# Mean embedding and projection: a tile's columns moved to VectorE, and three steps of the start and of every tile put elsewhere

## The chip, the core and the metric

The kernel runs on one core of a Trainium2 chip. The metric is device time in microseconds, the median of several executions. PE is TensorE's matmul, PEld its weight load, DVE is VectorE, ACT ScalarE, POOL GpSimd, SP SyncE (it issues DMAs).

## The reference

```python
valid = sequence_ids < emb_table.shape[0]            # ids (1024, 200), table (12500, 512)
safe_ids = jnp.where(valid, sequence_ids, 0)
seq_emb = emb_table[safe_ids] * valid[..., None]
denom = jnp.maximum(valid.sum(axis=1, keepdims=True), 1.0)
user_repr = seq_emb.sum(axis=1) / denom              # (1024, 512)
logits = user_repr @ proj_w + proj_b                 # (512, 12500), (12500,)
```

Ids run from 35 to 109962, so about one in nine is valid (some 23 of 200). All arrays are float32 (ids int32).

## The kernel before

Users are split into 8 tiles of 128 (one per partition), the 12500 items into 25 weight tiles of 500. VectorE sorts each tile's valid ids to the front (`sort`, five rounds of eight). POOL then gathers table rows, one indirect DMA per column: column j of tile t brings the j-th valid row of all 128 users, for 26 columns (c = 26 t + j), into a ring of 12 buffers. Some users have more than 26 valid ids; the tile's rest of these (up to 128 rows) is listed by three small PE products (`list_rest`), gathered as one more column into `rest_rows`, and added by `sum_rest`. For more still there is a loop behind a branch on a count (`add_further`), which every tile has to test; `sum_further` waits for the columns so far and calls it.

A column is added to its tile's sum in one of two ways. PE multiplies it by a diagonal mask built on ScalarE and accumulates in the PSUM tile `turned` (`sum_column`); VectorE multiplies by the mask and adds into `sums` (`add_column`). `ON_PE` says which columns PE takes: all of tile 0, 18 to 25 of tile 1, 24 and 25 of tile 2. VectorE then makes the mean from `sums` and ScalarE's `rest_mean` (`mean_of`), PE transposes it into `turned` (`turn`, L758), and ScalarE and VectorE split it into a high and a low half.

The projection runs in 200 units (one weight tile by one user tile), in the order of a list made when the program is built: tile 0 alone first (units 0 to 9), then further tiles join at units 10, 22, 35, 51, 65, 81 and 98 (`joined`). A unit is 12 matmuls (L829) into one of 6 PSUM banks. ScalarE or VectorE moves a bank out (`move_out`; ScalarE's units get their bias by one more matmul, L834, VectorE adds `bias_sb`, L635), and SP stores it. VectorE also makes the low halves of weight tiles (`w_low`, L620).

Every engine has a queue of its own, in the order of the loops over units; `column_due` spreads a tile's columns over the units before it joins. POOL's queue holds nothing but gathers from 5.8 us on. SP's holds, first, ids, weight tiles 0 to 4 and four bias tiles, then per unit its store, weight load and bias load. At the end of tile 1's and tile 2's VectorE columns stands `sum_further`, three units before the tile joins; `mean_of` follows one unit later for tiles 1 and 2 and at once for the others. `rest_share` and `sum_rest` come two units ahead for tiles with columns on PE, three for the others.

Of the kernel before, what the change touches and what calls it, by code (L numbers as in the profile page):

```python
# [5 lines left out]
def mean_embedding_projection(nc, ids, table, proj, bias, out, FAST=26,  # L6
# [8 lines left out]
    TILES = USERS // P  # L15
# [11 lines left out]
    RAW, SPLIT, BIAS, ROWS, PLACED, BANKS = 2, 5, 4, 12, 2, 6  # L27
    CH = 2

    ON_PE, DIAGS = ((0, FAST), (18, FAST), (24, FAST)), 4  # L30
    RAW_MORE, MORE_LOADS = 2, 16
    ACT_TILES, BOTH_TILES = 1, 5
    PART_AT = (0, 32, 64)
    BIAS_ROWS = PART_AT[-1] + NB
# [25 lines left out]
    UNITS = len(units)  # L60
# [21 lines left out]
    dve_last = [max((c for c in range(FAST * t, FAST * (t + 1)) if not by_pe[c]), default=None) for t in range(TILES)]  # L82
    assert all(at % CH == 0 for pair in ON_PE for at in pair)

    GATHER_LEAD = 5
    LATE_LOAD, REST_FIRST_AT, OPENED = 7, 18, SPLIT - 1

# [9 lines left out]
    ONCE = RAW + RAW_MORE  # L97
# [13 lines left out]
    with ctx:  # L111
# [163 lines left out]
            return first_diags[c] if c < FAST else diag[:, nth[c] % DIAGS]  # L275

        def list_of(t):
            return turned if t else first_list

        @block.sync  # L280
        def _(sp):
            def load_w(q):
                if raw_last[q] is not None:
                    sp.wait_ge(s_w_lo, raw_last[q] + 1)
                sp.dma_start(raw(q), w_view[:, :, bass.ts(q % NB, BW)]).then_inc(s_raw[raw_slot[q]], 16)

            def load_bias(i):

                if i >= BIAS:
                    wait_moved(sp, late_last[i - BIAS])  # L290
                sp.dma_start(bias_sb[:, i % BIAS], bias_view[late[i] % NB:late[i] % NB + 1].to_broadcast([P, BW])).then_inc(
                    s_bias[i % BIAS], 16)

            def store(g):
                r, q, first, n = stores[g]
                wait_moved(sp, r + n - 1)
                sp.dma_start(out_view[:, first:first + n, bass.ts(q % NB, BW)],
                             stage[:, g % STAGE, 0:n]).then_inc(s_stored[g % STAGE], 16)

            sp.dma_start(ids_sb[:, 0], ids_view[:, 0]).then_inc(s_ids0, 16)  # L300
            sp.dma_start(ids_sb[:, 1:], ids_view[:, 1:]).then_inc(s_ids, 16)
            for q in range(RAW):
                load_w(q)
            sp.wait_ge(s_bias_zero, 1)
            for at in PART_AT:
                sp.dma_start(bias_raw[at:at + NB], bias_view).then_inc(s_bias_raw, 16)
            first_loads = [q for q in range(LOADS) if raw_last[q] is None or raw_last[q] < SPLIT]
            for q in first_loads[RAW:]:
                if q == LATE_LOAD:
                    sp.wait_ge(s_rows[(FAST - 1) % ROWS], 16 * ((FAST - 1) // ROWS + 1))  # L310
                load_w(q)
                if q == ONCE:
                    for i in range(BIAS):
                        load_bias(i)
            sp.wait_ge(s_bias_parts, 3)
            for r in range(UNITS):
                for g in range(len(stores)):
                    if stores[g][0] + stores[g][3] - 1 == r:
                        store(g)
                for q in range(len(first_loads), LOADS):  # L320
                    if split_due[raw_last[q]] == r:
                        load_w(q)
                for i in range(BIAS, len(late)):
                    if r == late_last[i - BIAS]:
                        load_bias(i)
            for i in range(STAGE):
                sp.wait_ge(s_stored[i], 16 * len(range(i, len(stores), STAGE)))
# [162 lines left out]
        def _(dve):  # L490
# [90 lines left out]

            def sum_further(t):
                if t:
                    dve.wait_ge(s_summed, nth[dve_last[t]] + 1)
                else:
                    dve.memset(sums[:], 0.0).then_inc(s_cleared, 1)
                    dve.wait_ge(s_cleared, 1)
                add_further(t)
# [8 lines left out]
                                         ALU.add).then_inc(s_mean, 1)  # L597

            def mean_of(t):
                dve.wait_ge(s_turned, t)  # L600
                dve.wait_ge(s_rest_mean, t)
                dve.scalar_tensor_tensor(mean[:], sums[:], inv_count[:, t:t + 1], rest_mean[:], ALU.mult,  # L602
                                         ALU.add).then_inc(s_mean, 1)
# [120 lines left out]
            for r in range(UNITS):  # L724
                if not by_act[r]:
                    move_out(r)
                if r and r in joined[:-1]:
                    fill_slots(joined.index(r) + 1)
                for q in range(SPLIT, LOADS):
                    if split_due[q] == r:  # L730
                        w_low(q)
                for t in range(1, len(ON_PE)):
                    if r + 2 == joined[t]:
                        mean_of(t)
                for c in range(FAST, COLS):
                    if not by_pe[c] and column_due(c) == r and c >= FAST + 4:
                        add_column(c)
                        t, j = divmod(c, FAST)
                        if 1 < t and t + 1 < TILES and j in SORT_NEXT:
                            sort(t + 1, SORT_NEXT.index(j))  # L740
                        if t + 1 < TILES and j == (SELECT_NEXT if t > 1 else 15):
                            choose(t + 1)
                for t in range(1, TILES):
                    if r + MEAN_AHEAD == joined[t]:
                        sum_further(t)
                        if t >= len(ON_PE):
                            mean_of(t)
                if r + TURN_AHEAD + 1 in joined[1:]:
                    mean_low(joined.index(r + TURN_AHEAD + 1))

        @block.tensor
        def _(pe):
# [8 lines left out]
            def list_rest(t):  # L761

                pe.wait_ge(s_select, 2 * t + 2)
                if t:
                    pe.wait_ge(s_mean_lo, t)
                place_in = list_of(t)
                nc.tensor.transpose(place_in[:, 0:P], select[:], ident[:])
                nc.tensor.matmul(place_in[:, VALUES:VALUES + REST], select[:], top[:, t, FAST:SORTED], start=True, stop=True)
                nc.tensor.matmul(place_in[:, PLACE:PLACE + 1], select[:], before[:, t:t + 1],
                                 start=True, stop=True).then_inc(s_listed, 1)  # L770
# [25 lines left out]
            for c in pe_columns[0]:  # L796
                if c == REST_FIRST_AT:
                    sum_rest(0)
                sum_column(c)
            turn(0)  # L800
            pe.wait_ge(s_bias_parts, 3)
            pe.wait_ge(s_pick, 2)
            for r in range(UNITS):
                for t in range(1, TILES):
                    if r == (column_due(FAST * t + ON_PE[t][0]) if t < len(ON_PE) else joined[t] - REST_AHEAD):
                        sum_rest(t)
                for c in range(FAST, COLS):
                    if by_pe[c] and column_due(c) == r:
                        sum_column(c)
                if r + TURN_AHEAD in joined[1:]:  # L810
                    turn(joined.index(r + TURN_AHEAD))
                q, t = units[r]
                if r == 0:
                    pe.wait_ge(s_w_lo, OPENED)
                if r == first_unit[q]:
                    pe.wait_ge(s_w_lo, q + 1)
                if r >= BANKS:
                    wait_moved(pe, r - BANKS)
                bank = acc[:, r % BANKS, 0:BW]
                if r == joined[t]:  # L820
                    pe.wait_ge(s_mean_hi, t + 1)
                for part in range(3):
                    if r == joined[t] and part == 2:
                        pe.wait_ge(s_mean_lo, t + 1)
                    for k in range(K):
                        hi, lo = (x[:, t, k * P:(k + 1) * P] for x in (mean_hi, mean_lo))
                        high, low = (x[:, q % SPLIT, k] for x in (w_hi, w_lo))
                        first, second = ((hi, high), (hi, low), (lo, high))[part]
                        last = nc.tensor.matmul(bank, first, second, start=part + k == 0,  # L829
                                                stop=part == 2 and k == K - 1 and not by_act[r])  # L830
                if r in joined[:-1]:
                    list_rest(t + 1)
                if by_act[r]:
                    last = nc.tensor.matmul(bank, pick[:, q % NB:q % NB + 1].to_broadcast([BIAS_ROWS, P]), bias_parts[:],  # L834
                                            start=False, stop=True)
                last.then_inc(s_product, 1)
# [22 lines left out]
```

## Time and profile before

| what | us |
|---|---|
| median of 3 runs (lowest, highest) | 640.46 (640.25, 640.85) |
| profiled execution, whole / span | 641.41 / 639.7 |
| PE busy | 609.9 (95%) |
| PEld busy | 477.1 (75%) |
| DVE busy | 407.6 (64%) |
| POOL busy | 230.1 (36%) |
| ACT busy | 145.5 (23%) |
| DMA | 158.31 MB, mean 247 GB/s |

Busy shares are means over a start in which gathers, sorting and splitting go on and a long second half of nothing but units. The granted clock is TensorE's, 1.00 being 2.4 GHz and 0.5 being 1.2 GHz.

### The profile page before, as it was taken

The numbers are of one execution on the slowest core, as the hardware profiler recorded it, in microseconds if no ns is written. First come the engines' busy times: TensorE is split into PE (matmuls) and PEld (weight loads), VectorE is DVE, ScalarE is ACT, GpSimd is POOL, SyncE is SP. The second block draws the span as 40 slices with busy tenths as digits, with TensorE's granted clock in tenths as the row PEclk, the third lists the DMA queues.
The fourth block names the chain that finished last, engine by engine and source line by source line (L and its number), as shares of the span: only waits on it lengthen the run. The fifth ranks groups of instructions, "written<-read, shape, count | busy, mean of one in ns | idle before, by whom it ended". The sixth has DMA issues, their size and how long they took to land.

```text
span 639.7 us, 7596 instructions
## 1 busy us (share of the span) xinstructions
PE 609.9 (95%) x2602; PEld 477.1 (75%) x2602; DVE 407.6 (64%) x723; ACT 145.5 (23%) x161; POOL 230.1 (36%) x227
## 2 busy tenths in 40 slices
PE   1989899999999999999999999999999999999997
PEld 0327558678787777788788788888888888888886
DVE  7988959989879698797785554332333333344442
ACT  8917525131140131300200221111011111211210
POOL 5777877767765667565550000000000000000000
PEclk9999999989999999999999999999999999999999
DMA  9989999989999889798793398454555555566632
GB/s 310 388 292 371 391 369 314 367 285 323 309 327 314 272 289 309 231 329 246 233 334 112 97 290 276 122 177 157 170 173 177 176 177 176 170 192 203 219 124 106
DMA packets 77703, 158.31 MB, mean 247 GB/s; under 512 B 9287, under 2 KB 65042, under 8 KB 77658
## 3 DMA queue, kind: packets, MB, share of 16 engines
q1 hardware_dynamic: 60378, 110.30, 51.0%
q0 software_dynamic: 17280, 47.47, 23.2%
q8 instruction: 21, 0.34, 0.2%
q14 instruction: 24, 0.20, 0.1%
HBM read 115.70 MB, written 51.20 MB: 261 GB/s over the span
## 4 chain that ended last, share of the span: by engine, by line
PE 76%; DVE 14%; issue 5%; DMA 3%; DVEq 1%; ACT 0%; POOL 0%; POOLq 0%
PE acc L829 72%; DVE sums L557 6%; DMA rows<-in_L_rec_emb_table_dram,index 3%; DVE w_lo L620 3%; PE turned L783 2%; DVE key L514 1%; DVE top L510 1%; PE turned L758 1%; PE acc L834 1%; PE turned L775 1%; DVE stage L635 1%; DVE mean L602 0%; POOL rows L349 0%; DVEq L255 0%; DMA ids_sb<-in_r_sequence_ids_dram 0%
## 5 line engine op out<-in xcount | busy, mean ns | idle before, releaser
L349 POOL DMA_INDIRECT rows<-in_L_rec_emb_table_dram,index x208 | 220.4, 1060 | 94.7 <-issue 57.0
L829 PE MATMUL acc<-w_hi,mean_hi 128*128 128x500 f32 x800 | 224.7, 402 | 0.8 <-ACT mean_hi L434 0.8
L635 DVE TENSOR_TENSOR stage<-acc,bias_sb 128x500 f32<-128x500 f32 x162 | 109.2, 676 | 181.8 <-PE acc L829 181.5
L829 PE MATMUL acc<-w_lo,mean_hi 128*128 128x500 f32 x800 | 214.7, 390 | 0.0
L829 PE MATMUL acc<-w_hi,mean_lo 128*128 128x500 f32 x800 | 214.3, 390 | 0.2 <-DVE mean_lo L607 0.2
L829 PEld LDWEIGHTS acc<-w_hi,mean_lo 128*128 128x128 f32 x800 | 150.7, 189 | 32.2 <-DVE mean_lo L607 1.2
L829 PEld LDWEIGHTS acc<-w_lo,mean_hi 128*128 128x128 f32 x800 | 150.8, 189 | 31.4
L829 PEld LDWEIGHTS acc<-w_hi,mean_hi 128*128 128x128 f32 x800 | 150.3, 189 | 32.0 <-issue 4.3
L557 DVE SCALAR_TENSOR_TENSOR sums<-rows,mask,sums 128x512 f32<-128x512 f32 x165 | 124.0, 752 | 8.2
L418 ACT ACTIVATE w_hi<-w_raw 128x2000 fp32r<-128x2000 f32 x39 | 72.9, 1875 | 232.6 <-PE acc L829 215.8
L620 DVE TENSOR_TENSOR w_lo<-w_raw,w_hi 128x1000 fp32r<-128x1000 f32 x74 | 85.2, 1193 | 10.5 <-ACT w_hi L418 10.5
L409 ACT ACTIVATE stage<-acc 128x500 f32<-128x500 f32 x38 | 22.2, 586 | 82.8 <-PE acc L834 82.8
L445 ACT ACTIVATE rest_mean<-turned,inv_count 128x512 f32<-128x512 f32 x7 | 4.8, 689 | 77.6 <-PE turned L775 68.9
L783 PE MATMUL turned<-rows,diags_at_hi 128*128 128x512 f32 x30 | 16.0, 692 | 1.3 <-DMA rows<-in_L_rec_emb_table_dram,index 1.3
L510 DVE MAX8 top<-key 128x8 f32<-128x200 f32 x40 | 14.6, 366 | 0.7
L834 PE MATMUL acc<-bias_parts,pick 89*128 89x500 bf16 x38 | 14.6, 385 | 0.0
L602 DVE SCALAR_TENSOR_TENSOR mean<-sums,inv_count,rest_mean 128x512 f32<-128x512 f32 x7 | 5.3, 751 | 14.2 <-issue 7.1
L514 DVE MATCH_REPLACE8 key<-top,key 128x200 f32<-128x200 f32 x40 | 14.1, 352 | 0.0
L783 PEld LDWEIGHTS turned<-rows,diags_at_hi 128*128 128x128 f32 x30 | 6.5, 224 | 10.0 <-issue 7.6
L783 PE MATMUL turned<-rows,diag 128*128 128x512 f32 x20 | 10.2, 624 | 3.7 <-ACT diag L402 2.1
L783 PE MATMUL turned<-rows,diags_at_lo 128*128 128x512 f32 x22 | 11.5, 628 | 1.7 <-DMA rows<-in_L_rec_emb_table_dram,index 1.4
L434 ACT ACTIVATE mean_hi<-turned 128x512 fp32r<-128x512 f32 x8 | 4.8, 597 | 34.8 <-PE turned L758 34.8
(106 smaller groups left out, 180.4 us busy)
## 6 DMA issues: line engine op xcount, KB each, us to landing
out_dram<-stage SPq DMA_DIRECT2D x200, 250.0 KB, 3.7
w_raw<-in_L_rec_proj_w_dram SPq DMA_DIRECT2D x39, 1000.0 KB, 6.5
bias_sb<-in_L_rec_proj_b_dram SPq DMA_DIRECT2D x39, 250.0 KB, 4.6
raw_at_hi<-in_L_rec_proj_w_dram SPq DMA_DIRECT2D x4, 1000.0 KB, 10.1
rows<-in_L_rec_emb_table_dram,index POOLq DMA_INDIRECT x208, 5.8
raw_at_lo<-in_L_rec_proj_w_dram SPq DMA_DIRECT2D x3, 1000.0 KB, 14.3
stage<-in_L_rec_proj_w_dram SPq DMA_DIRECT2D x1, 1000.0 KB, 26.2
ids_sb<-in_r_sequence_ids_dram SPq DMA_DIRECT2D x1, 700.0 KB, 4.6
```

Of the source, the lines that this page charges most:

```text
L349: return pool.indirect_dma_start(out=dst, out_offset=None, in_=table, in_offset=bass.IndirectOffsetOnAxis(ap=column, axis=0), bounds_check ...
L409: nc.scalar.activation(stage[:, g % STAGE, r - stores[g][0]], acc[:, r % BANKS, 0:BW], ACT.Copy).then_inc(s_moved_by_act, 1)
L418: nc.scalar.activation(w_hi[:, q % SPLIT], raw(q), ACT.Copy).then_inc(s_w_hi, 1)
L510: dve.max(eight, key[:]).then_inc(s_sort, 1)
L514: dve.match_replace(key[:], eight, key[:], -1.0).then_inc(s_sort, 1)
L557: dve.scalar_tensor_tensor(sums[:], rows[:, c % ROWS], mask[:, t, j:j + 1], sums[:], ALU.mult, ALU.add).then_inc(s_summed, 1)
L620: low = dve.tensor_tensor(w_lo[:, q % SPLIT, at:at + half], raw(q)[:, at:at + half], high, ALU.subtract)
L635: dve.tensor_tensor(stage[:, g % STAGE, r - stores[g][0]], acc[:, r % BANKS, 0:BW], bias_sb[:, i % BIAS], ALU.add).then_inc(s_moved_by_dve, 1)
L758: last = nc.tensor.transpose(turned[:, k * P:(k + 1) * P], mean[:, k * P:(k + 1) * P], ident[:])
L783: nc.tensor.matmul(turned[:], diagonal_of(c), rows[:, c % ROWS], start=j == 0, stop=j == FAST - 1).then_inc(s_added, 1)
L829: last = nc.tensor.matmul(bank, first, second, start=part + k == 0, stop=part == 2 and k == K - 1 and not by_act[r])
L834: last = nc.tensor.matmul(bank, pick[:, q % NB:q % NB + 1].to_broadcast([BIAS_ROWS, P]), bias_parts[:], start=False, stop=True)
```

## The change

Tile 2 has no columns on PE any more; VectorE adds all 26 and, as `ON_PE` has one entry less, its mean is made three units ahead, right behind its last column, and its rests are added three units ahead too. The test for further rows moves from behind a tile's last VectorE column to behind column 20 (16 for tile 1), and `mean_of` waits for the last column instead. The four first bias loads move on SP from behind weight tile 4 to unit 3. Tile 1's list of rests moves on PE from unit 0 to ahead of column 21 of tile 0, and from `turned` into the PSUM bank of unit 5, which then waits until the list was read.

```diff
-    ON_PE, DIAGS = ((0, FAST), (18, FAST), (24, FAST)), 4
+    ON_PE, DIAGS = ((0, FAST), (18, FAST)), 4
+    FURTHER_BEHIND, LIST_FIRST_AT, BIAS_DUE = 20, 21, 3
+    further_behind = [min(FURTHER_BEHIND, pe_columns[t].start - 2) if pe_columns[t] else FURTHER_BEHIND
+                      for t in range(TILES)]
         def list_of(t):
-            return turned if t else first_list
+            return turned if t > 1 else first_list
...
-                if q == ONCE:
+            sp.wait_ge(s_bias_parts, 3)
+            for r in range(UNITS):
+                if r == BIAS_DUE:
                     for i in range(BIAS):
                         load_bias(i)
-            sp.wait_ge(s_bias_parts, 3)
-            for r in range(UNITS):
...
             def sum_further(t):
                 if t:
-                    dve.wait_ge(s_summed, nth[dve_last[t]] + 1)
+                    dve.wait_ge(s_summed, nth[FAST * t + further_behind[t]] + 1)
             def mean_of(t):
+                dve.wait_ge(s_summed, nth[dve_last[t]] + 1)
...
                         add_column(c)
                         t, j = divmod(c, FAST)
+                        if j == further_behind[t]:
+                            sum_further(t)
...
                 for t in range(1, TILES):
-                    if r + MEAN_AHEAD == joined[t]:
-                        sum_further(t)
-                        if t >= len(ON_PE):
-                            mean_of(t)
+                    if t >= len(ON_PE) and r + MEAN_AHEAD == joined[t]:
+                        mean_of(t)
...
             def list_rest(t):
                 pe.wait_ge(s_select, 2 * t + 2)
-                if t:
+                if t == 1:
+                    pe.wait_ge(s_placed, 1)
+                    pe.wait_ge(s_rest_index, 1)
+                elif t:
                     pe.wait_ge(s_mean_lo, t)
...
                 if c == REST_FIRST_AT:
                     sum_rest(0)
+                if c == LIST_FIRST_AT:
+                    list_rest(1)
                 sum_column(c)
...
+                if r == BANKS - 1:
+                    pe.wait_ge(s_placed, 2)
+                    pe.wait_ge(s_rest_index, 2)
...
-                if r in joined[:-1]:
+                if r and r in joined[:-1]:
                     list_rest(t + 1)
```

## Rows read from the trace of the kernel before

**Rows 1.** The page, part 4: shares of the chain that ended last, by engine.

```profile
PE 76%; DVE 14%; issue 5%; DMA 3%; DVEq 1%; ACT 0%; POOL 0%; POOLq 0%
```

**Rows 2.** PE's waits: who waited for whom, us in total, times, longest.

```profile
PE turned L758 <- DVE mean L602: 3.6, 3, 1.9
PE turned L783 <- DMA rows<-in_L_rec_emb_table_dram,index: 4.3, 6, 1.3
```

**Rows 3.** Timeline of PE at tile 2: start, us, operation, [idle before <-releaser].

```profile
121.80 1.02 PE L775 MATMUL turned<-rest_rows,placed 128*128 128x512 f32 x2
122.66 1.92 PE L783 MATMUL turned<-rows,diag 128*128 128x512 f32 x4
124.01 1.47 PE L829 MATMUL acc<-w_hi,mean_hi 128*128 128x500 f32 x4
...
129.39 0.66 PE L758 MATMUL turned<-ident,mean 128*128 128x128 f32 x4 [1.88 <-DVE mean L602]
```

**Rows 4.** Stretches: length, busy PE, PEld, DVE, ACT, POOL, clock, DMA share, GB/s.

```profile
76.00:80.00 4.00, 2.81 (x6) 1.06 (x6) 3.96 (x7) 2.69 (x8) 3.10 (x3) 1.00 1.04 393
96.30:127.10 30.80, 30.80 (x131) 23.55 (x130) 29.72 (x54) 11.56 (x13) 23.48 (x23) 1.00 0.98 338
128.00:132.00 4.00, 2.61 (x11) 2.25 (x12) 3.13 (x6) 0.79 (x2) 3.01 (x4) 0.82 1.00 357
132.00:136.00 4.00, 4.00 (x16) 3.23 (x15) 3.77 (x10) 0.00 (x0) 3.00 (x3) 0.75 0.95 326
```

**Rows 5.** Timeline of DVE from tile 2's list to its mean.

```profile
96.33 0.22 DVE L572 TENSOR_SCALAR rank<-turned,own_slot 128x1 f32<-128x1 f32 x1 [1.18 <-PE turned L769]
...
99.39 0.68 DVE L635 TENSOR_TENSOR stage<-acc,bias_sb 128x500 f32<-128x500 f32 x1
...
123.38 2.46 DVE L557 SCALAR_TENSOR_TENSOR sums<-rows,mask,sums 128x512 f32<-128x512 f32 x3
...
126.34 0.75 DVE L557 SCALAR_TENSOR_TENSOR sums<-rows,mask,sums 128x512 f32<-128x512 f32 x1
128.58 0.75 DVE L602 SCALAR_TENSOR_TENSOR mean<-sums,inv_count,rest_mean 128x512 f32<-128x512 f32 x1 [1.49 <-issue]
```

**Rows 6.** Timelines of DVE and PE at tile 6, and of PE at 7.

```profile
302.46 0.68 DVE L635 TENSOR_TENSOR stage<-acc,bias_sb 128x500 f32<-128x500 f32 x1 [2.23 <-PE acc L829]
...
305.27 0.75 DVE L602 SCALAR_TENSOR_TENSOR mean<-sums,inv_count,rest_mean 128x512 f32<-128x512 f32 x1 [1.47 <-issue]
...
306.08 0.66 PE L758 MATMUL turned<-ident,mean 128*128 128x128 f32 x4 [1.02 <-DVE mean L602]
...
355.15 0.66 PE L758 MATMUL turned<-ident,mean 128*128 128x128 f32 x4 [0.73 <-DVE mean L602]
```

**Rows 7.** Timelines of PE and DVE at tile 3.

```profile
162.96 1.02 PE L775 MATMUL turned<-rest_rows,placed 128*128 128x512 f32 x2
163.41 1.48 PE L829 MATMUL acc<-w_hi,mean_hi 128*128 128x500 f32 x4
...
168.92 0.75 DVE L602 SCALAR_TENSOR_TENSOR mean<-sums,inv_count,rest_mean 128x512 f32<-128x512 f32 x1 [0.95 <-DVE sums L557]
...
169.73 0.66 PE L758 MATMUL turned<-ident,mean 128*128 128x128 f32 x4
```

**Rows 8.** DVE's waits.

```profile
DVE mean L602 <- ACT rest_mean L445: 6.2, 1, 6.2
```

**Rows 9.** Timeline: ACT's copy of tile 1's list, PE's unit 5.

```profile
54.25 0.28 ACT L439 ACTIVATE placed<-turned 128x128 f32<-128x128 f32 x1 [3.00 <-DVE rest_index L579]
...
64.73 1.25 PE L829 MATMUL acc<-w_hi,mean_hi 128*128 128x500 f32 x4
```

**Rows 10.** Timeline of SP's DMA issues.

```profile
7.58 14.30 SPq L291 DMA_DIRECT2D bias_sb<-in_L_rec_proj_b_dram  x4
```

**Rows 11.** POOL's gathers by line, from 54 to 80 us, then 24 to 40 us.

```profile
L349 POOL DMA_INDIRECT rows<-in_L_rec_emb_table_dram,index x17 | 21.1, 1240 | 5.2 <-issue 4.6 <-DVE sums L557 0.6
...
L349 POOL DMA_INDIRECT rows<-in_L_rec_emb_table_dram,index x12 | 12.0, 997 | 3.7 <-issue 2.4 <-PE turned L783 1.2
```

More of the change, by code:

```diff
@@ L83, in mean_embedding_projection @@
     assert all(at % CH == 0 for pair in ON_PE for at in pair)
+    further_behind = [min(FURTHER_BEHIND, pe_columns[t].start - 2) if pe_columns[t] else FURTHER_BEHIND
+                      for t in range(TILES)]
+    assert all(by_pe[FAST * t + j] is False and j >= FAST - ROWS for t, j in enumerate(further_behind) if t)
     GATHER_LEAD = 5
```

## The prediction

> **What bounds the kernel now.** I read the page's chain of waits first, for the engine on which the end hangs. It gives TensorE (PE) three quarters of the span and VectorE (DVE) most of the rest [rows 1]. After that I asked where PE stands still, because a microsecond of PE waiting, once its units run, is a microsecond of the end. PE's waits name two causes that this change touches: the transposes of a mean (L758) wait 3.6 us for VectorE in three places, and the diagonal products of table rows (L783) wait 4.3 us for gathers in six places [rows 2]. Third, the timelines around those places.
>
> At tile 2 PE leaves the sum of the rests at 121.80, does two columns from 122.66, starts unit 20 at 124.01, finishes it at 129.39 - 1.88 = 127.51 and then waits 1.88 us for the mean [rows 3]. VectorE is what is late there. From 96.30 to 127.10 it is busy for 29.72 of 30.80 us [rows 4], and its last wait for another engine, 1.18 us for PE's list of tile 2, ends at 96.33 [rows 5]. So from 96.33 until the mean at 128.58 this stage is one uninterrupted VectorE queue, and PE has time to spare in it. At tiles 6 and 7 the picture is the other one: VectorE itself waits 2.23 us for a product, adds the last column, tests for further rows and only then makes the mean; PE stands 1.02 us at 306.08 and 0.73 us at 355.15 for it [rows 6]. 1.88 + 1.02 + 0.73 are the 3.6 us of PE's waits, so tiles 3, 4 and 5 have no such wait of size.
>
> **The change part by part.** Durations are of the profiled execution, which took 641.41 us (span 639.7 and 1.7 around it), 0.95 us over the median of 640.46. I add the terms to 641.41 and take 0.95 off at the end.
>
> *Tile 2's two columns.* PE loses two columns. At tile 3, which has none, a unit follows the sum of the rests by 163.41 - 162.96 = 0.45 us [rows 7]; at tile 2 by 124.01 - 121.80 = 2.21 [rows 3]. So PE is 1.76 us earlier at the end of unit 20. This is worth nothing by itself: PE would only wait longer, since VectorE is the late one. ScalarE's two diagonals go too, off the path. VectorE gains two columns. Three in a row take 2.46 us from the first's start to the last's end [rows 5], so the pitch is (2.46 - 0.75) / 2 = 0.855, and two more are 1.71 us on a queue with no gap. Their rows were gathered for PE before 124.01, so VectorE doesn't wait for them at 127 or later. Term: +1.71 at tile 2's mean.
>
> *The test for further rows, tile 2.* It moves from behind the last column to behind column 20. It costs VectorE the time from the end of the last column, 126.34 + 0.75 = 127.09, to the mean at 128.58: 1.49 us, with some 0.1 that any dependent step takes [rows 5]. It waits for column 20's sum before it loads its register, so it empties the queue at the new place as at the old, and behind it stand the remaining columns and bank moves. VectorE has no idle time there to hide it [rows 4]. Term: 0. The same step takes 0.95 at tile 3 [rows 7], so at the new place it could be 0.54 cheaper; the other end is as dear as any of its rows, 1.49. Range -0.5 to +0.1.
>
> *The test, tiles 6 and 7.* Behind column 20 it lies in time in which VectorE waits for products anyway (2.23 us just ahead of the last column [rows 6]). The mean then starts right after the last column, about 1.4 us earlier than 305.27, and PE needs it only 1.02 us earlier. Both waits go: -1.02 - 0.73 = -1.75. What is late next is PE itself. At tiles 4 and 5 PE doesn't wait for the mean, so 0. At tile 1 the mean waits 6.2 us for ScalarE's share of the rests [rows 8], which hides the test at either place.
>
> *The test, tile 3.* Mean and transposes follow with no gap: the mean ends at 168.92 + 0.75 = 169.67, the transposes begin at 169.73 [rows 7]. The stage is VectorE-bound like tile 2's, and the test stays in it. Term 0, from -0.1 to +0.5 (0.95 against 1.49).
>
> *The clock behind tile 2's wait.* From 128 to 136 the granted clock is 0.82 and then 0.75 [rows 4], that is, 1.2 GHz for part of it, after PE's wait of 1.88 us: 4 x 0.18 + 4 x 0.25 = 1.72 us of PE work lost. The wait grows to 1.88 + 1.76 + 1.71 = 5.35 us. No row shows so long a wait between units. At the least the loss goes (-1.72, since the shorter waits for rows before 87 us show a clock of 1.00, as in 76 to 80 [rows 4]); at the most it doubles. The nearest row is the same place, so I take the same loss: 0.
>
> *Tile 1's list and the waits that come with it.* PE makes it at column 21 of tile 0, where the rows of the gathers keep PE waiting (the 4.3 us [rows 2]), so three small products fit in. It waits for tile 0's list to have been used and for the choice on VectorE, both done long before; behind it in PE's queue stand only the last five columns. The new wait at unit 5 (at 64.73) is for a copy that ScalarE began at 54.25 [rows 9]: ten microseconds of cover. Unit 0 gets shorter by them, but PE waits for gathered rows ahead of unit 8 in any case, so the gain is lost there. Term: 0.
>
> *The first bias loads.* SP spends 14.30 us from 7.58 on issuing four of them [rows 10]. Without them the first loads and gathers have the DMA engines more to themselves, and unit 0 may start up to a microsecond earlier, which again ends at the rows that unit 8 waits for. At the new place, unit 3, they stand on SP ahead of that unit's store and weight load and all later ones, whose banks and buffers are used again many units on; their own first user is VectorE's bank move at 99.39 [rows 5], 34 us after even unit 5 (64.73) began. Term: 0.
>
> *What sets unit 8.* The gathers leave POOL one behind another. From 54 to 80 they take 1240 ns each, from 24 to 40 they take 997 [rows 11]: 17 x 0.243 = 4.1 us lost, beside seven pairs of low-half subtractions (L620) on VectorE, 0.6 us a pair. If VectorE's work shifts against POOL's, a pair more or less is hit: 0, from -0.6 to +0.6.
>
> **Sum.** 641.41 + 1.71 (columns) + 0 (test, tile 2) + 0 (clock) + 0 (tile 3) + 0 (start) - 1.75 (tiles 6 and 7) = 641.37; less 0.95: 640.4 us. Gain and loss cancel.
>
> **The rivals.** *A: the test at tile 2 leaves the path.* If VectorE has a gap near column 20 after all (PE's earlier units, or a longer wait for a bank), the test is swallowed and the mean comes only 1.71 - 1.39 = 0.32 later. For it: at tiles 6 and 7 it is so. Against it: 29.72 of 30.80 us busy [rows 4]. Time: 641.41 + 0.32 - 1.75 - 0.95 = 639.0.
>
> *B: the longer wait costs more clock.* It lies at unit 21; it decides if TensorE, after a wait nearly three times as long, works at 1.2 GHz for twice as long. Price: another 1.72, which VectorE doesn't hide, because it waits for the list that PE makes at the head of tile 2's units. Time: 640.4 + 1.7 = 642.1. For it: the drop was there after 1.88 us already. Against it: part of a low stretch may pass while PE still waits, which costs nothing.
>
> The Trainium skill, "TensorE: Matmul & The Clock Gate", section "What's actually happening", says that the throttled state is the default and that activity releases it. The 0.82 and 0.75 behind PE's wait agree [rows 4]. By that rule the loss is sure after 5.35 us of waiting and less sure after 1.88; if the median run before was without it, the rule would give 642.1 where the rows of the profiled execution give 640.4.
>
> *C: the bias loads hurt where they go.* From 76 to 80 the DMA share is 1.04 at 393 GB/s [rows 4]. Four loads write 1 MB, 1.0 / 0.393 = 2.6 us of it. If the last two gathers of tile 1 are held up by that much, unit 8 and all behind it come 2.6 us later: 643.0. It decides if the gathers queue behind the loads. Against it: the DMA engines are as full now, and gathers pass.
>
> **How the numbers follow.** Forecast 0.52, A 0.22, B 0.16, C 0.10. What this measurement can tell from no change is 0.2%, 1.3 us. The forecast's own range is 639.2 to 641.8, from its open terms (test, tile 3, start, part of the clock), so of its 0.52 I count 0.40 within, 0.08 faster and 0.04 slower. A gives 0.18 faster and 0.04 within; B 0.12 slower and 0.04 within; C 0.09 slower and 0.01 within. Faster 0.26, same 0.49, slower 0.25. The range reaches to A with its cheapest test and to B, and stops short of C: 638.5 to 642.6.
>
> **What would show it.** In the profile after: PE's two columns at tile 2 gone; the wait of L758 for tile 2's mean about 5 us instead of 1.88, and that mean about 1.7 us later than 128.58; a granted clock below 1 right after it; no wait of L758 at tiles 6 and 7; unit 8 at the same time as before to about half a microsecond. I am wrong if tile 2's mean is not later (A), if the low clock behind it lasts clearly longer (B), if tile 1's last columns wait longer for rows (C), or if the waits at tiles 6 and 7 stay.

## The result, and the profile after

The changed kernel takes 641.87 us (median of 20 runs, 640.57 to 643.30), the kernel before 640.60 (20 runs, 640.08 to 641.00). The ratio is 1.0020, 95% interval 1.0014 to 1.0026: 1.3 us slower (0.9 to 1.7), where I had forecast no change. The profiled executions hide this: 641.41 us before and 641.37 after. The one of before lies above all 20 runs of before, the one of after half a microsecond under the median of after.

In the profile after, the lines of before have moved: the turn of a mean is L763 (was L758), the mean L607, a column on VectorE L561, the unit's products L842, the columns on PE L791, the sum of the rests L783, the bank move L640. The shares of the chain have hardly changed [rows 1]:

```profile
PE 77%; DVE 13%; DMA 4%; issue 4%; ACT 0%; DVEq 0%; POOL 0%; POOLq 0%
```

PE's waits (total, times, longest), against [rows 2]. Three waits for a mean have become two, and one of them is three times as long; the waits for rows are shorter, and one for a diagonal stands beside them:

```profile
PE turned L763 <- DVE mean L607: 5.9, 2, 5.7
PE turned L791 <- ACT diag L406: 3.5, 1, 3.5
PE turned L791 <- DMA rows<-in_L_rec_emb_table_dram,index: 2.8, 5, 1.0
```

PE at tile 2, against [rows 3]. The unit follows the rests by 0.46 us, with no columns between. PE ends it at 125.24, 2.27 sooner than before, and then waits until 130.92, so the turn is 1.53 later. The four products behind it take 2.02 us where the same four took 1.48 at 119.00:

```profile
118.54 1.02 PE L783 MATMUL turned<-rest_rows,placed 128*128 128x512 f32 x2
119.00 1.48 PE L842 MATMUL acc<-w_hi,mean_hi 128*128 128x500 f32 x4
...
130.92 1.11 PE L763 MATMUL turned<-ident,mean 128*128 128x128 f32 x4 [5.68 <-DVE mean L607]
131.69 2.02 PE L842 MATMUL acc<-w_hi,mean_hi 128*128 128x500 f32 x4
```

Stretches (columns as in [rows 4]): VectorE's from tile 2's list to its mean, and the two in which the granted clock was 0.82 and 0.75 before. It is now 0.56 and 0.59, near the lower of the two levels (1.2 GHz); in the first of them PE works for only 1.08 of 4.00 us:

```profile
95.80:130.11 34.31, 29.44 (x128) 22.94 (x127) 31.55 (x56) 11.55 (x12) 25.33 (x25) 0.98 1.00 357
128.00:132.00 4.00, 1.08 (x5) 1.08 (x6) 3.68 (x6) 0.00 (x0) 3.09 (x4) 0.56 0.92 318
132.00:136.00 4.00, 4.00 (x13) 3.21 (x12) 3.79 (x11) 0.60 (x1) 3.04 (x4) 0.59 0.96 342
```

VectorE over that time, against [rows 5]. The test for further rows now stands between column 20 (122.89) and a bank move, and VectorE is idle for 1.27 us there instead of 1.49 just ahead of the mean. From the list's answer to the mean are 34.31 us, 2.06 more than the 32.25 before:

```profile
95.80 0.22 DVE L576 TENSOR_SCALAR rank<-turned,own_slot 128x1 f32<-128x1 f32 x1 [1.19 <-PE turned L777]
...
96.60 0.76 DVE L561 SCALAR_TENSOR_TENSOR sums<-rows,mask,sums 128x512 f32<-128x512 f32 x1
97.26 0.36 DVE L514 MAX8 top<-key 128x8 f32<-128x200 f32 x1
...
101.68 2.47 DVE L561 SCALAR_TENSOR_TENSOR sums<-rows,mask,sums 128x512 f32<-128x512 f32 x3
104.06 0.36 DVE L514 MAX8 top<-key 128x8 f32<-128x200 f32 x1
...
122.89 0.75 DVE L561 SCALAR_TENSOR_TENSOR sums<-rows,mask,sums 128x512 f32<-128x512 f32 x1
124.92 0.68 DVE L640 TENSOR_TENSOR stage<-acc,bias_sb 128x500 f32<-128x500 f32 x1 [1.27 <-issue]
125.51 3.32 DVE L561 SCALAR_TENSOR_TENSOR sums<-rows,mask,sums 128x512 f32<-128x512 f32 x4
...
129.33 0.75 DVE L561 SCALAR_TENSOR_TENSOR sums<-rows,mask,sums 128x512 f32<-128x512 f32 x1
130.11 0.75 DVE L607 SCALAR_TENSOR_TENSOR mean<-sums,inv_count,rest_mean 128x512 f32<-128x512 f32 x1
```

Tile 6 on VectorE, then tiles 6 and 7 on PE, against [rows 6]. The mean follows the last column with no test between, and neither turn has a wait any more:

```profile
304.59 0.68 DVE L640 TENSOR_TENSOR stage<-acc,bias_sb 128x500 f32<-128x500 f32 x1 [1.75 <-PE acc L842]
305.19 0.75 DVE L561 SCALAR_TENSOR_TENSOR sums<-rows,mask,sums 128x512 f32<-128x512 f32 x1
305.97 0.75 DVE L607 SCALAR_TENSOR_TENSOR mean<-sums,inv_count,rest_mean 128x512 f32<-128x512 f32 x1
```

```profile
307.03 0.60 PE L763 MATMUL turned<-ident,mean 128*128 128x128 f32 x4
...
355.14 0.60 PE L763 MATMUL turned<-ident,mean 128*128 128x128 f32 x4
```

### The profile page after: what moved, and what is told of

Its sections match the earlier page's. It is cut to its first block, busy times and chain, and to the rows that moved or that the text cites. A ratio compares the mean times of both kernels' runs of the same rounds, so it can differ in the third digit from the quotient of the medians.

```text
span 639.6 us, 7590 instructions
## 1 busy us (share of the span) xinstructions
PE 607.6 (95%) x2598; PEld 477.7 (75%) x2598; DVE 409.5 (64%) x725; ACT 145.0 (23%) x159; POOL 229.2 (36%) x227
## 4 chain that ended last, share of the span: by engine, by line
PE 77%; DVE 13%; DMA 4%; issue 4%; ACT 0%; DVEq 0%; POOL 0%; POOLq 0%
PE acc L842 72%; DVE sums L561 5%; DMA rows<-in_L_rec_emb_table_dram,index 4%; DVE w_lo L625 3%; PE turned L791 2%; DVE key L518 1%; DVE top L514 1%; PE turned L783 1%; PE acc L847 1%; PE turned L763 1%; DVE stage L640 0%; DMA ids_sb<-in_r_sequence_ids_dram 0%; DVE count L652 0%; ACT w_hi L422 0%; POOL rows L353 0%
## 5 line engine op out<-in xcount | busy, mean ns | idle before, releaser
L640 DVE TENSOR_TENSOR stage<-acc,bias_sb 128x500 f32<-128x500 f32 x162 | 109.3, 676 | 183.3 <-PE acc L842 181.7
L842 PE MATMUL acc<-w_hi,mean_hi 128*128 128x500 f32 x800 | 225.1, 403 | 0.8 <-ACT mean_hi L438 0.8
L842 PE MATMUL acc<-w_lo,mean_hi 128*128 128x500 f32 x800 | 214.7, 390 | 0.0
L842 PE MATMUL acc<-w_hi,mean_lo 128*128 128x500 f32 x800 | 213.8, 389 | 0.2 <-DVE mean_lo L612 0.2
L842 PEld LDWEIGHTS acc<-w_hi,mean_hi 128*128 128x128 f32 x800 | 150.7, 190 | 32.0 <-issue 4.3
L842 PEld LDWEIGHTS acc<-w_hi,mean_lo 128*128 128x128 f32 x800 | 150.4, 188 | 32.0 <-DVE mean_lo L612 1.1
L842 PEld LDWEIGHTS acc<-w_lo,mean_hi 128*128 128x128 f32 x800 | 150.8, 189 | 31.4
L561 DVE SCALAR_TENSOR_TENSOR sums<-rows,mask,sums 128x512 f32<-128x512 f32 x167 | 125.5, 752 | 15.3 <-issue 6.7
L791 PE MATMUL turned<-rows,diags_at_hi 128*128 128x512 f32 x30 | 15.5, 661 | 1.8 <-DMA rows<-in_L_rec_emb_table_dram,index 1.8
L791 PEld LDWEIGHTS turned<-rows,diags_at_hi 128*128 128x128 f32 x30 | 6.1, 214 | 10.5 <-issue 5.4
L791 PE MATMUL turned<-rows,diag 128*128 128x512 f32 x16 | 9.1, 721 | 4.0 <-ACT diag L406 3.5
L353 POOL DMA_INDIRECT rest_rows<-in_L_rec_emb_table_dram,rest_index x8 | 8.2, 1031 | 12.9 <-DVE sums L561 7.9
L763 PE MATMUL turned<-ident,mean 128*128 128x128 f32 x32 | 5.4, 296 | 7.3 <-DVE mean L607 5.9
```

The lines of the kernel that those rows point to most:

```text
L353: return pool.indirect_dma_start(out=dst, out_offset=None, in_=table, in_offset=bass.IndirectOffsetOnAxis(ap=column, axis=0), bounds_check ...
L561: dve.scalar_tensor_tensor(sums[:], rows[:, c % ROWS], mask[:, t, j:j + 1], sums[:], ALU.mult, ALU.add).then_inc(s_summed, 1)
L640: dve.tensor_tensor(stage[:, g % STAGE, r - stores[g][0]], acc[:, r % BANKS, 0:BW], bias_sb[:, i % BIAS], ALU.add).then_inc(s_moved_by_dve, 1)
L763: last = nc.tensor.transpose(turned[:, k * P:(k + 1) * P], mean[:, k * P:(k + 1) * P], ident[:])
L791: nc.tensor.matmul(turned[:], diagonal_of(c), rows[:, c % ROWS], start=j == 0, stop=j == FAST - 1).then_inc(s_added, 1)
```

## The experiments

Two theories stood at the start. *Q*: tile 2's columns cost more than the earlier test gives back, by VectorE's later mean and by the low clock behind PE's longer wait. *S*: the moves at the start (bias loads, tile 1's list) cost it. The table is of use for all runs; a *turn* is the transposing of a tile's mean on PE. From each profile: VectorE's time from tile 2's list to its mean; from turn 1 to turn 2 on PE; PE's wait ahead of turn 2; from turn 2 to turn 3, where PE waits at most 0.76 us for the next mean, so that a low clock shows; from turn 3 to turn 7, which holds the tests at tiles 4 to 7. Then the ratio to the kernel before by the timed runs, 0.001 being 0.64 us. Last, how far the profiled run lies from the median of its own kernel, in us: as far as the differences that are argued here. The largest of these go with where turn 1 begins (88.40 and 88.80 in e10 and e9; 90.07, 90.46 and 90.48 in e4, e11 and e1), so only stretches from there on are compared. Each is of a single execution, and VectorE's idle time at tile 2's test alone is anything from 1.23 to 1.81 us in them.

| kernel | list to mean | turn 1 to 2 | wait at 2 | turn 2 to 3 | turn 3 to 7 | ratio (95%) | profiled run, from median |
|---|---|---|---|---|---|---|---|
| before | 32.25 | 39.81 | 1.88 | 40.34 | 185.42 | 1 | +0.81 |
| after | 34.31 | 41.88 | 5.68 | 40.99 | 183.23 | 1.0020 (1.0014–1.0026) | -0.50 |
| e1 after, tile 2 back on PE | 32.03 | 39.59 | 0.52 | 39.75 | 183.26 | 0.9968 (0.9956–0.9980) | +1.00 |
| e2 before, tile 2 on VectorE | 34.53 | 42.11 | 5.90 | 41.13 | 185.44 | 1.0060 (1.0047–1.0073) | +0.37 |
| e3 after, wait filled | 34.66 | 42.23 | 1.15 | 39.66 | 183.27 | 0.9999 (0.9988–1.0009) | +0.51 |
| e4 after, banks on ScalarE | 32.72 | 40.29 | 2.97 | 40.82 | 183.25 | 0.9979 (0.9968–0.9989) | +1.35 |
| e5 before, start moved | 32.00 | 39.57 | 1.26 | 39.45 | 185.55 | 0.9995 (0.9986–1.0004) | +0.66 |
| e6 before, test moved | 32.51 | 40.08 | 0.99 | 39.65 | 183.24 | 0.9982 (0.9973–0.9991) | -0.41 |
| e7 before, wait filled | 32.05 | 39.61 | none | 39.37 | 185.36 | 1.0001 (0.9992–1.0010) | -0.29 |
| e8 e1 and e4 | 30.16 | 38.83 | none | 39.63 | 183.30 | 0.9950 (0.9936–0.9963) | 0.00 |
| e9 after, columns short | 33.24 | 40.80 | 4.57 | 40.33 | 183.24 | 0.9997 (0.9987–1.0007) | -1.13 |
| e10 e1, VectorE work added | 33.89 | 41.45 | 2.68 | 40.69 | 183.32 | 1.0009 (1.0001–1.0018) | -1.19 |
| e11 after, no test at tile 2 | 32.93 | 40.48 | 4.26 | 41.57 | 183.31 | 0.9994 (0.9985–1.0002) | +1.77 |
| e12 after again | 34.34 | 41.89 | 5.67 | 40.66 | 183.31 | 1.0020 (1.0008–1.0031) | -0.64 |

**The parts one by one: e1, e2, e5, e6.** e1 takes only tile 2's columns out of the change, e2 does nothing but them:

```diff
-    ON_PE, DIAGS = ((0, FAST), (18, FAST)), 4
+    ON_PE, DIAGS = ((0, FAST), (18, FAST), (24, FAST)), 4
```

> The changed kernel with tile 2's columns 24 and 25 given back to TensorE (its mean again two units ahead); the test, the bias loads and the list stay moved. Theory Q (VectorE's queue): tile 2's two columns are all that costs, and the moved test gives back what the profiles show at tiles 5 to 7, 2.1 us. Then 640.6 - 2.1 = 638.5 us. Rival S (the start): the moved bias loads or list cost about the 1.3 us that the whole change cost, through later gathers for unit 8; then tile 2 is neutral and this kernel stays between 640 and 642 us.

> The kernel before with only ON_PE changed: VectorE adds all of tile 2's columns and its mean comes three units ahead, the test behind the last column as before. Theory Q: tile 2's mean about 2 us later and PE's wait about 5.5 us instead of 1.9, with 0.5 to 1.4 us more lost at 1.2 GHz behind it: 640.6 + 2.0 + 0.5 to 1.4 = 643.1 to 644.0 us. Rival S: the two columns cost nothing net, 640.6 plus or minus 0.5 us.

e1 took 638.31 us against 640.33, e2 644.11, 0.1 beyond its range. So the columns alone cost 3.8 us (0.0060), and without them the change gains 2.0; put into the rest of the change they cost 3.3 (1.0020 against 0.9968). S is refuted: what is left of the change when the columns are back is faster than before.

e5 makes only the moves at the start (the bias loads at unit 3, tile 1's list at column 21 with its waits), e6 only that of the test:

```diff
-                    dve.wait_ge(s_summed, nth[dve_last[t]] + 1)
+                    dve.wait_ge(s_summed, nth[FAST * t + further_behind[t]] + 1)
...
+                        if j == further_behind[t]:
+                            sum_further(t)
```

> Before, with the first bias loads and tile 1's list moved as in the change, and nothing else of it. Theory Q (tile 2's queue and clock cost, the earlier test gains): unit 8 starts 0.52 us earlier in the changed kernel's trace, and tile 2's mean, which VectorE sets, follows from tile 1's end, so 0 to -0.5 us, 639.8 to 640.4 us against 640.3 before. Rival S (the start costs): +1 us, about 641.3. Rival R (the start is what gained the 2 us by which the change with tile 2's columns put back beats before): 638.3 us.

> Before, with the test for further rows moved behind column 20 (behind an earlier one where TensorE adds the columns) and nothing else of the change. Theory Q: the waits ahead of turns 6 and 7 (1.02 and 0.73 us before) go, and tile 2's own test leaves the place just ahead of its mean, where it cost 1.49 us, for one in mid-queue, where it costs about 1.3: -1.75 to -2.1 us, 638.2 to 638.6 us. Rival R (the start gained the 2 us): 640.0 to 640.4 us.

e5: 639.94 against 640.52, not to be told from no change (+0.3 to -0.9 us). e6: 639.39, that is -1.2 us (-0.6 to -1.7), less than the 1.75 to 2.1 expected, though its profile shows what the theory says: turn 3 to 7 is 2.18 shorter. The profile of before is not the one to measure it by (more on that below). Against e7's, which is before without its wait at tile 2, turn 1 to 2 is 0.47 longer in e6 (the test took 1.81 us there, 1.27 in e7), turn 2 to 3 0.28 longer and turn 3 to 7 2.12 shorter: together 1.4 us, within the interval. Rival R, that the start gained the 2 us, fell.

**The clock: e3 and e7.** In both, PE gets products of a unit whose sums are overwritten, in place of its wait at tile 2, and the columns stay where they are. e3 adds 22 to the changed kernel, e7 adds 7 to the one before:

```diff
+                if r + TURN_AHEAD == joined[2]:
+                    wait_moved(pe, r - BANKS)
+                    pe.wait_ge(s_w_lo, q + 1)
+                    for _ in range(22):
+                        nc.tensor.matmul(acc[:, r % BANKS, 0:BW], mean_hi[:, t, 0:P], w_hi[:, q % SPLIT, 0],
+                                         start=True, stop=True)
```

> The changed kernel with 22 more matmuls of unit 21 (about 5 us at 2.4 GHz) ahead of tile 2's transposes, in the wait for its mean; they are overwritten by the unit's own. The mean comes no sooner, only the granted clock behind the wait should stay at 1.00. Theory K (the clock is a large part): what PE lost at 1.2 GHz after the wait, 2.1 us in the profiled execution, comes back: 641.9 - 2.1 = 639.8 us. Rival (the clock is cheap, because VectorE is the late engine in the stage that follows): less than 0.7 us comes back, 641.2 us or more.

> Before, with seven further matmuls of a unit, whose sums are overwritten, in TensorE's queue ahead of tile 2's turn, so that it works through most of the 1.88 us for which it waited there. Theory Q: the granted clock of the stretch 128 to 140 us is 1.00 in every run; 12 of before's 20 runs have a mean clock of 1.000 as it is, so the median gains 0 to 0.4 us, 639.9 to 640.4 us. Rival (the low clock costs before about as much as the changed kernel, 1.7 us, in its typical run): 638.6 us.

e3: 640.08, ratio 0.9999, nearer to theory K's 639.8 than to its rival's 641.2. The whole loss is gone, although VectorE's mean is not sooner (list to mean 34.66) and PE does more. Its timeline of PE and its stretch behind the turn:

```profile
125.08 5.20 PE L825 MATMUL acc<-w_hi,mean_hi 128*128 128x500 f32 x22
131.42 0.66 PE L763 MATMUL turned<-ident,mean 128*128 128x128 f32 x4 [1.15 <-DVE mean L607]
131.83 1.16 PE L848 MATMUL acc<-w_hi,mean_hi 128*128 128x500 f32 x4
```

```profile
132.00:136.00 4.00, 4.00 (x20) 3.30 (x18) 3.69 (x12) 0.60 (x1) 3.09 (x4) 1.00 0.98 363
```

PE does the four products in 1.16 us where they took 2.02, at a granted clock of 1.00, and turn 2 to turn 3 falls from 40.99 to 39.66. e7, the same cure for the kernel before, gains nothing: 640.67 against 640.52, ratio 1.0001 (0.9992 to 1.0010), a little over the 640.4 expected at most. So the kernel before has no such loss in its typical run, or one of at most 0.5 us. Two stretches of e7:

```profile
76.00:80.00 4.00, 3.44 (x5) 1.53 (x6) 3.96 (x7) 1.70 (x6) 3.13 (x3) 0.62 1.04 391
132.00:136.00 4.00, 3.98 (x21) 3.03 (x20) 3.79 (x10) 0.00 (x0) 3.08 (x4) 1.00 1.02 344
```

The clocks of the runs say the same: 12 of the 20 runs of before beside e1 to e4 have a mean granted clock of 1.000 (their median is 640.18, that of the other eight, at 0.997, 640.51), while all 20 of the changed kernel stand at 0.989 or 0.992, and the 12 of e3 at 0.994 to 0.997. In the two later sets of runs of before 23 of 62 stand at 0.999 or 1.000, with medians 0.2 and 0.3 under those of the others; a mean below that needn't come from behind turn 2, since e7's profile has 0.997 and its low stretch from 76 to 80 us (0.62), where PE waits for rows anyway. The profiled execution of before was one with a drop behind turn 2. e5, whose tile 2 is before's, shows one without: 1.26 us of wait, a clock of 1.00 from 128 to 140, 39.45 from turn 2 to 3.

**VectorE's load and PE's queue apart: e4, e9, e10, e11.** e4 moves the banks of tile 1's units on ScalarE, with the bias by a product on PE:

```diff
-    ACT_TILES, BOTH_TILES = 1, 5
+    ACT_TILES, BOTH_TILES = 2, 5
```

> The changed kernel with all banks of units 10 to 21 moved out by ScalarE (ACT_TILES 2 instead of 1): VectorE loses six bank moves of 0.6 us ahead of unit 22, PE gains six bias matmuls of 0.23 us. Theory Q: five of the six stand ahead of tile 2's mean, which comes some 3 us sooner; PE's wait falls from 5.7 to about 1.5 us and most of the low clock goes with it: 641.9 - 3 - 1 to 2 = 637 to 638 us. Rival (the mean is held by something other than VectorE's queue, such as the last gathered rows): the mean doesn't move and the time is that of the changed kernel or 1 us more.

639.31, ratio 0.9979: VectorE's stretch gets 1.59 us shorter (34.31 to 32.72), and turn 2 comes 1.59 sooner after turn 1. That misses the 3 us and the 637 to 638 us expected. In part it is that 12 columns instead of 10 now follow right behind another column (the price of that is worked out below) and that the test took 0.18 longer; the low clock stayed in the profiled run (2.97 us of wait, turn 2 to 3 in 40.82). What ends PE's wait at tile 2 is still VectorE's mean.

In e9 VectorE adds columns 24 and 25 in their first element alone; in e10 PE has the two columns and VectorE two further operations of their size:

```diff
+                    w = 1 if t == 2 and j in (24, 25) else K * P
+                    dve.scalar_tensor_tensor(sums[:, 0:w], rows[:, c % ROWS, 0:w], mask[:, t, j:j + 1], sums[:, 0:w],
...
```

```diff
+                    if t == 2 and j == 23:
+                        for i in range(2):
+                            dve.wait_ge(s_extra, i)
+                            dve.scalar_tensor_tensor(fb_rows[:, 0], rows[:, c % ROWS], mask[:, t, j:j + 1], sums[:],
+                                                     ALU.mult, ALU.add).then_inc(s_extra, 1)
```

> The changed kernel, in which VectorE adds tile 2's columns 24 and 25 in their first element alone (the other 511 are left out of the sums): both engines are then spared the two columns. Theory Q (the price is VectorE's later mean, and the low clock after the longer wait adds to it): turn 1 to turn 2 takes 39.6 us as where TensorE has the columns, TensorE's wait is about 2.3 us, that is 0.52 plus the 1.74 by which its queue is shorter, and what it loses beyond that is at most the 1.0 us of the low clock: 638.3 to 639.3 us with before at 640.3. Rival T (TensorE's shorter queue is itself what costs, by the wait and the clock): 640.3 us or more.

> The changed kernel with columns 24 and 25 back on TensorE, and two further operations on VectorE, alike in kind and size to two columns, ahead of tile 2's column 23, written to an unused place: both engines have the work. Theory Q: tile 2's mean comes 1.7 to 2.1 us later than without them, TensorE waits 0.52 plus that, about 2.4 us, and the low clock after it costs 0 to 1.0 us: 640.0 to 641.4 us against 638.3 without them, before at 640.3. Rival T (TensorE's queue sets turn 2, not VectorE's): 638.3 to 638.8 us.

e10 came as Q has it: 641.27, 1.86 us more from list to mean than e1, 0.94 more from turn 2 to 3; 2.8 together, 2.6 by the ratios (1.0009 against 0.9968). Of the 1.86, 0.48 is the test, by the rows of e1 and e10:

```profile
126.37 1.62 DVE L561 SCALAR_TENSOR_TENSOR sums<-rows,mask,sums 128x512 f32<-128x512 f32 x2 [1.28 <-issue]
124.71 1.61 DVE L567 SCALAR_TENSOR_TENSOR sums<-rows,mask,sums 128x512 f32<-128x512 f32 x2 [1.76 <-issue]
```

e9 missed: 640.53, where Q said 638.3 to 639.3 and T, that PE's shorter queue itself costs, 640.3 or more. Its profile shows both causes, T's as the smaller. Turn 1 to 2 is 1.21 longer than in e1, and all of it is VectorE's (33.24 against 32.03); turn 2 to 3 is 0.58 longer, behind a wait of 4.57 and at a low clock, as T has it. Together 1.8 us, beside 1.9 by the ratios (0.0029). The profiled run of e9 isn't a typical one, though: it lies 1.13 under the median, at a mean clock of 0.995, where 7 of the 12 runs stand at 0.992 or less. T's share can be larger in those; no run here shows it. Q's 39.6 from turn 1 to 2 was an error of mine: shortening the columns by all but one element takes away only about half of their price on VectorE. VectorE, PE and the stretches behind the turn in e9:

```profile
124.65 0.68 DVE L641 TENSOR_TENSOR stage<-acc,bias_sb 128x500 f32<-128x500 f32 x1 [1.28 <-issue]
125.25 2.79 DVE L562 SCALAR_TENSOR_TENSOR sums<-rows,mask,sums 128x512 f32<-128x512 f32 x4
127.94 0.68 DVE L641 TENSOR_TENSOR stage<-acc,bias_sb 128x500 f32<-128x500 f32 x1
128.54 0.21 DVE L562 SCALAR_TENSOR_TENSOR sums<-rows,mask,sums 128x1 f32<-128x1 f32 x1
```

```profile
129.60 1.12 PE L764 MATMUL turned<-ident,mean 128*128 128x128 f32 x4 [4.57 <-DVE mean L608]
```

```profile
128.00:132.00 4.00, 2.40 (x8) 2.15 (x9) 3.68 (x9) 0.60 (x1) 3.00 (x3) 0.64 1.03 303
132.00:136.00 4.00, 4.00 (x18) 3.29 (x18) 3.86 (x10) 0.00 (x0) 2.99 (x3) 0.94 0.96 345
```

The other half is the order of the queue. The kernel spreads a tile's VectorE columns over the units, and with 26 instead of 24 more of them stand one right behind another. The rows of after show what that costs: a column followed by something else hands over after 97.26 - 96.60 = 0.66 us, while three in a row take 104.06 - 101.68 = 2.38, that is 0.86, 0.86 and 0.66. From list to mean there are 6 such successions before, 10 after and 10 in e9, but 5 in e1. For e9 against e1 that is 5 x 0.20 = 1.0 of the 1.21 us. That the order and not something else does it rests on this count alone; no run changed the order by itself.

e11 leaves tile 2's test out of the changed kernel:

```diff
-                        if j == further_behind[t]:
+                        if t != 2 and j == further_behind[t]:
```

> The changed kernel without tile 2's test for further rows (a register load and a branch on VectorE; the test is left out). Theory Q: the 1.27 us that VectorE stood at the test after column 20 go from the way to the mean, and the low clock costs up to 0.4 us less since TensorE waits 4.4 us and not 5.7: 639.9 to 640.4 us against 641.6, before at 640.3. Rival (VectorE would have waited there for the gathered rows anyway): 641.3 to 641.6 us.

640.29 us, beside 641.58 of the changed kernel on the same chip (e12): 1.3 us (1.7 by the ratios), and 1.41 less from list to mean. Its place in the middle of the queue hid nothing of the test.

**The changed kernel again, and a faster version: e12, e8.**

> The changed kernel again, beside the runs of before of this chip: 1.0014 to 1.0026 of before, 641.2 to 642.0 us where before takes 640.3, with a mean granted clock of 0.989 to 0.992.

> The changed kernel with tile 2's columns 24 and 25 back on TensorE and with the bank moves of tile 1's units on ScalarE. Theory Q: what VectorE is spared matters only where TensorE still waits for it: 0.52 us ahead of turn 2 and 0.72 us ahead of turn 3, so 637.1 to 638.2 us against 638.3 without the bank moves on ScalarE. Rival (spared VectorE work is worth what it was in the changed kernel, 1.3 us): 637.0 us or less.

e12 gave 641.58 against 640.49, ratio 1.0020 as at first, 11 of 12 runs at a clock of 0.989 or 0.992. e8 (tile 2's columns back on PE, tile 1's banks on ScalarE, the rest of the change kept) is the fastest: 637.02 us, 3.2 us under the kernel before by the ratio. PE's timeline around turn 2 has no wait left, and the clock of the stretch is full:

```profile
127.55 0.39 PE L847 MATMUL acc<-bias_parts,pick 89*128 89x500 bf16 x1
127.77 0.60 PE L763 MATMUL turned<-ident,mean 128*128 128x128 f32 x4
```

```profile
128.00:132.00 4.00, 4.00 (x21) 3.23 (x20) 3.79 (x12) 1.67 (x3) 3.08 (x4) 1.00 0.87 246
```

Its time is at the edge between what Q and the rival expected, 637.1 and 637.0, and doesn't tell them apart.

## Why the prediction was wrong

*The step that failed* is the clock term together with the 0.95 us taken off at the end. For the profiled execution the sum said 641.37, and the profiled execution after took 641.37. That is luck: turn 1 begins 0.54 sooner, turn 1 to 2 is 2.07 longer, 2 to 3 0.65 longer and 3 to 7 2.19 shorter, none of them as forecast, and they cancel. I then took 0.95 off, because the profiled run of before lay that much above its median. But most of that 0.95 was the low clock itself: turn 2 to 3 took 40.34 us there and 39.37 when e7 filled the wait, 0.97 more. By "I take the same loss: 0" I had the loss on both sides, and by the subtraction I took it off both. It comes off only one: before, more than half the runs beside e1 to e4 are without any drop; after, both profiles have it behind 5.7 us of wait, and the mean clocks of all 20 runs fit. Turn 2 to 3 is 40.66 and 40.99 us in the two profiles of the changed kernel, and 39.37 to 39.75 in the six whose clock stayed at 1.00 there: 0.9 to 1.6 us, and e3 shows that the loss of 1.3 us goes with it. With the clock term at +1.3 and the rest as it was, the sum is 641.7, where 641.87 was measured.

This was rival B, to which I gave 0.16. Its price there, 1.72, was too high as read from the window: a part of the low stretch passes while PE still waits (from 128 to 132 PE works for 1.08 of 4.00 us), which the text itself had against it. The 1.00 from 76 to 80, on which the cheapest end of the term rested, doesn't hold from run to run either: that stretch has 0.62 in e7. The rule cited beside it, from the Trainium skill, "TensorE: Matmul & The Clock Gate", section "What's actually happening", that activity is what releases the throttled clock, agrees with these traces: 0.56 and 0.59 behind 5.68 us without work, 1.00 where 5.20 us of it are filled by products whose sums nobody uses. The sentence "if the median run before was without it" was the condition that held, and the times in front of me could have told me: a profiled run 0.95 us over a median whose runs span 0.6 us is not a typical run.

*Tile 2's columns*: right in kind, some 0.6 short. VectorE had no gap, PE's 1.76 us were worth nothing, and the mean came 2.06 later, not 1.71, although the test took 1.27 for 1.49. Without VectorE's idle time at the test, list to mean is 30.70 to 30.78 us in before, e1, e5, e6 and e7, and 33.03 to 33.07 in after, e3 and e12: the columns cost 2.3. I priced two columns at the pitch of columns in a row; the change also put more of the old columns in a row: 2 x 0.66 + 4 x 0.20 = 2.1, an estimate from the rows of after.

*The test at tile 2*: right, 0 (1.27 idle for 1.49, within what it varies by from run to run). Rival A is refuted by e11: the test is on the path wherever it stands in that queue. *Tile 3*: turn 3 still follows its mean, with 0.26 of wait; no gain to be seen.

*Tiles 6 and 7*: right in kind, both waits gone. Turn 3 to 7 is 2.19 us shorter in the profile against the 1.75 of the two waits: turn 5 to 6 is 1.18 shorter for its 1.02, 6 to 7 0.96 for its 0.73. e6 measured 1.2 (0.6 to 1.7) for the test as a whole, tiles 2 and 3 with it.

*The start*: right. Unit 8 begins at 85.70 instead of 86.22, 0.52 us sooner and within the 0.6 I had allowed, and e5 measures no difference. Rival C is refuted by it, and so is S.

The parts close if e7's profile stands for before without the drop: from turn 1 to turn 7 the two profiles of the changed kernel take 266.10 and 265.86 us, that one 264.34. With e5's -0.3 for the start this makes +1.2 to +1.5 us, and 0.9 to 1.7 were measured.

What stays open: turn 1 begins between 88.40 and 90.48 us in these profiles with no clear relation to the edits. And only the profiled runs show where their low clock lies, so how many of the runs of before have it behind turn 2 isn't known.

## What to carry to other kernels

Before taking a profile as the ground of a forecast, ask whether its execution is a typical one: find what in it (a stretch of low clock, above all) accounts for its distance from the median, and carry that item on one side only. Where VectorE sets the end of a stage, work moved to it from TensorE can be paid twice, as here: by the later result, and by the lower clock behind the longer wait. Work that is moved should go to the engine with time to spare, as e8 does with the bank moves. And a chain of dependent operations on VectorE cost more here where they stood one behind another (0.86 us against 0.66): moving two can change the order of all.

## What the runs showed of the hardware that I had not expected

- The price of the low clock didn't follow the length of the wait: in the eight profiles that have it behind turn 2, one execution each, turn 2 to 3 took 40.33 to 41.57 us behind waits of 1.88 to 5.90 us, the most behind 4.26 (e11) and the least behind 4.57 (e9).
- A dependent VectorE column right behind another costs 0.86 us, and with another instruction between 0.66; one of a single element still takes 0.21 (e9).
- At a test of a loaded register with a branch VectorE stood idle for 1.23 to 1.81 us at tile 2 in the profiles of the kernels that have it: 1.27 to 1.81 in the middle of the queue, 1.23 to 1.63 at its end.
- The four bias loads took SP 14.30 us to issue at 7.58 [rows 10] and 2.85 at their new place, at 61.84.
